# A fused cross-attention, MLA and expert kernel: the queries' RMS factor applied in the softmax's scale, and a new order inside the MLA's head pairs

## The chip, the cores and the metric

The kernel runs on one core of a Trainium2 chip, as one program. The metric is the device time of one execution in microseconds, the median of three runs. The engines are TensorE (PE in the rows, with its weight loads as PEld), VectorE (DVE), ScalarE (ACT), GpSimd (POOL) and SyncE (SP), which issues most transfers. Each runs its own list of instructions in order, and they wait for one another on semaphores.

## The reference

`x` is 256 x 512. Three blocks follow one another, each with a layer norm in front and added to `x`: cross-attention over 4096 rows of context, a multi-head latent attention (MLA) with 16 causal heads, and a mixture of 48 kept experts. The change lies in the MLA, but for one instruction:

```python
q_lat = rms_norm(h @ w_qa.T, q_a_ln_w)              # 384 wide, one factor per row
kv = h @ w_kva.T                                    # 128 latent + 64 rotary
c = rms_norm(kv[..., :128], kv_a_ln_w)              # 128 wide, one factor per row
q = (q_lat @ w_qb.T)                                # per head 128 plain + 64 rotary
k_nope, v = split(c @ w_kvb.T)                      # per head 128 and 128
scores = (q_nope @ k_nope.T + rope(q_pe) @ rope(k_pe).T) * 192 ** -0.5
out = softmax(causal(scores)) @ v                   # then @ w_o.T, all heads
```

The factor of `rms_norm` is `rsqrt(mean(x * x) + eps)` of the row. Queries are rows of the scores, so a factor of a query's latent is a factor of that row of the scores.

## The kernel before

Products in fp32 are made of fp16 halves: an operand is scaled and rounded to a high half (mostly by ScalarE), the remainder is the low half (mostly VectorE, which waits for the high one), and TensorE adds three products, high-high, low-high and high-low.

*Opening.* The first transfers bring key weights `wk32` and context, chunk by chunk. ScalarE rounds chunk c (L471, semaphore `wk_hi`), VectorE makes the low half (`split_wk`), TensorE begins with chunk 0. Somewhat later `transpose_rows` (L1280) turns the normalised `x`, for which it waits for VectorE's L807. Cross-attention follows until 304 us; its exponentials are L531 and L577, whose bias and scale are both columns in SBUF.

*Latents.* The rows are two tiles, t = 0 and 1, of 128 tokens. `latents(t, ...)` writes 384 query and 128 key columns of a tile into one PSUM bank `lat_raw[t]`. ScalarE squares both parts with a sum (L609, L611, `ssq_ready`), VectorE adds epsilon (`add_eps`, L1043), POOL raises both columns to -0.5 (L439), behind the power of the tile's layer norm (L436), and `norm_latents` multiplies the raw latents with factor and weight, the query part in L1047 and the key part in L1049. Between these VectorE rotates the shared rotary keys (`rotate_keys`, L1033 and L1037). TensorE turns latents and keys (`turn_latents` L1512, `turn_keys` L1518), ScalarE and VectorE split the turned latents (L673, L1055). The projections of the first pair, `first_part(t, low, n)`, have n = 0 keys, 1 rotary queries and 2 plain queries; the queries of tile 0 (18 of 66 products) stand ahead of `turn_latents(1)`. Their results are evacuated by L663 (keys), L654 (queries), L1075 and L659 (rotary), with the low halves on VectorE in the order keys L1089, queries L1084, rotary L1080. The scores of pair 0 wait for all of them.

*Pairs.* The 16 heads are 8 pairs; pairs 0 to 6 are `mla_pair`, pair 7 is `mla_last_pair`. TensorE does for pair m: scores into `pO`; projections of pair m + 1 (queries and rotary, keys); six output products of pair m - 1 for tile 0 into `pD` (`out_product(..., 0)`); values of m + 1; six transposes of the probabilities (L1657), which wait for `p_ready`; six output products of pair m - 1 for tile 1 into `pP`; the weighted values, which wait for `pt_ready`. VectorE does: mask (L1103), row maximum (L1107, L1108), its negative times the scale (L1110), low half of the next key weights (L905), in pairs 4 to 6 the low half of an expert unit (L1094), reciprocal (L1116) and product with the probabilities (L1120), rotary product of the next queries (L1075), low halves (L1084, L1089, L1080), low half of the output weights (L1128), low half of the query weights two pairs ahead (L899), low half of the outputs (L1133). ScalarE does: next key weights (L511), four exponentials with row sums (L618), evacuation of the next queries and keys (L654, L663), output weights (L639), rotary high half (L659), evacuation of the turned probabilities (L625), query weights two pairs ahead (L506), outputs (L648) and values (L668), in pairs 3 to 5 also an expert unit's high half for the next pair (L687). In pair 0 alone (`start=True`) the output weights stand behind the turned probabilities. SP loads query weights and output weights of later pairs after `mkv_lo` and `wo_lo`.

Of the kernel before, what the change touches and what calls it, by code (L numbers as in the profile page):

```python
# [12 lines left out]
T, HID = 256, 512  # L13
# [34 lines left out]
def build(nc, a, out):  # L48
# [4 lines left out]
    with ctx:  # L53
# [66 lines left out]
        def take(n, dt=f32):  # L120
# [51 lines left out]
        epsv = take(TT)  # L172
        xsum = take(TT)
# [19 lines left out]
        latc = arena[:, pm_at:pm_at + TT * LAT].rearrange("p (t n) -> p t n", t=TT)  # L193
        kcos, ksin = (arena[:, woh_at + 256 * i:woh_at + 256 * i + 256].rearrange("p (t i d) -> p t i d", t=TT, i=2)
# [59 lines left out]
            wl_hi wl_lo bo_hi bo_ready xsq_ready xl1_ready lat_mm kpe_mm kpn_ready kpe_hi kpe_tr ssq_ready lvar_ready lrstd_ready latn_ready lat_tr lat_hi lat_lo mq_hi mq_lo mkv_hi mkv_lo kpe_ready  # L254
# [130 lines left out]
        def _(pool):  # L385
# [51 lines left out]
            for t in range(TT):  # L437
                pool.wait_ge(s["lvar_ready"], t + 1)
                pool.tensor_tensor(lrs[:, t], ssq[:, t], nhalf[:, :], ALU.pow).then_inc(s["lrstd_ready"], 1)  # L439
# [6 lines left out]
        def _(act):  # L446
# [22 lines left out]
            for c in range(HC):  # L469
                act.wait_ge(first_in[c], 32)  # L470
                act.activation(wk16[:, 0, c], wk32[:, c], ACT.Copy, scale=SW).then_inc(s["wk_hi"], 1)  # L471
# [155 lines left out]
            def mla_pair(m, p, proj=True, ahead=True, start=False):  # L627
# [6 lines left out]
                if start:  # L634
                    rope_hi(m + 1, 1 - p)
                    turned(m)
# [43 lines left out]
            mla_evac_k(0, 0, 1)  # L680
            mla_evac_q(0, 0, 3)
            rope_hi(0, 0)
# [1190 lines left out]
```

## Time and profile before

| | us |
|---|---|
| median of 3 runs (716.0 to 716.07) | 716.04 |
| the profiled execution, its own time | 716.18 |
| its span in the profile | 714.3 |
| TensorE busy | 700.1 (98%) |
| VectorE busy | 610.9 (86%) |
| ScalarE busy | 439.0 (61%) |
| POOL busy | 11.6 (2%) |

The granted clock of TensorE is 1.00 in every stretch shown below. A row of a timeline gives the start and the length in us, the engine, the line, the operation with output and inputs and, in brackets, how long the engine had been idle and who released it. Matmul ends are modelled, so that a matmul row's length holds a tail under which the next may start. A window row gives the stretch, its length, and busy time and instructions of PE, PEld, DVE, ACT and POOL in this order.

### The profile page before, as it was taken

The numbers are of one execution on the slowest core, as the hardware profiler recorded it, in microseconds if no ns is written. First come the engines' busy times: TensorE is split into PE (matmuls) and PEld (weight loads), VectorE is DVE, ScalarE is ACT, GpSimd is POOL, SyncE is SP. The second block draws the span as 40 slices with busy tenths as digits, with TensorE's granted clock in tenths as the row PEclk, the third lists the DMA queues.
The fourth block names the chain that finished last, engine by engine and source line by source line (L and its number), as shares of the span: only waits on it lengthen the run. The fifth ranks groups of instructions, "written<-read, shape, count | busy, mean of one in ns | idle before, by whom it ended". The sixth has DMA issues, their size and how long they took to land.

```text
span 714.3 us, 20505 instructions
## 1 busy us (share of the span) xinstructions
PE 700.1 (98%) x8725; PEld 455.7 (64%) x8725; DVE 610.9 (86%) x950; ACT 439.0 (61%) x610; POOL 11.6 (2%) x36
## 2 busy tenths in 40 slices
PE   8999999999999998998999999999999999999998
PEld 3555555555555554546777767777777777777775
DVE  5679999999999999877889977888888888888885
ACT  4778888787878887735677753444444344444442
POOL 3000000000000000010000000000000000000000
PEclk9999999999999999999999999999999999999999
DMA  8570101010110000032334403678777776777770
GB/s 322 175 276 3 62 3 62 3 61 10 54 25 39 3 3 3 3 128 98 112 121 155 161 1 105 224 215 250 220 246 222 242 239 227 245 225 243 230 238 32
DMA packets 29880, 94.44 MB, mean 132 GB/s; under 512 B 5824, under 2 KB 15088, under 8 KB 28400
## 3 DMA queue, kind: packets, MB, share of 16 engines
q1 hardware_dynamic: 28944, 92.31, 39.2%
q8 instruction: 57, 0.93, 0.6%
q10 hardware_dynamic: 864, 1.07, 0.4%
q14 instruction: 15, 0.12, 0.1%
HBM read 92.76 MB, written 0.57 MB: 131 GB/s over the span
## 4 chain that ended last, share of the span: by engine, by line
PE 91%; ACT 3%; DVE 3%; DMA 1%; issue 1%; POOL 0%; ACTq 0%; DVEq 0%
PE pS L1268 40%; PE pP L1268 30%; PE pO L1268 12%; PE pD L1268 8%; ACT arena L577 2%; DMA arena<-in_ctxT 1%; PE pO L1657 1%; ACT arena L618 0%; DVE xn L1183 0%; DVE xn L807 0%; POOL arena L439 0%; DVE bn L800 0%; DVE arena L1075 0%; DVE arena L790 0%; DVE arena L780 0%
## 5 line engine op out<-in xcount | busy, mean ns | idle before, releaser
L1268 PE MATMUL pS<-arena 128*128 128x256 f16 (+3 forms) x2185 | 253.5, 272 | 1.4 <-ACT arena L708 0.5
L1268 PEld LDWEIGHTS pS<-arena 128*128 128x128 f16 (+1 forms) x2185 | 213.4, 101 | 45.5 <-ACT arena L625 1.9
L1268 PE MATMUL pP<-arena 128*32 128x512 f16 (+1 forms) x2996 | 239.8, 380 | 0.2 <-ACT arena L471 0.2
L1268 PEld LDWEIGHTS pP<-arena 128*32 128x32 f16 (+1 forms) x2996 | 109.0, 97 | 102.0 <-issue 2.2
L531 ACT ACTIVATE arena<-pS,mblk 128x1024 f32<-128x1024 f32 x112 | 128.9, 1206 | 4.9 <-PE pS L1268 4.7
L1094 DVE SCALAR_TENSOR_TENSOR arena<-arena 128x1536 f16<-128x1536 f32 x72 | 126.1, 1752 | 0.8 <-ACT arena L687 0.8
L729 ACT ACTIVATE arena<-pS 128x256 f32<-128x256 f32 x72 | 27.6, 383 | 154.2 <-PE pS L1268 154.2
L1268 PE MATMUL pO<-arena 128*32 128x256 f32 (+6 forms) x1370 | 106.6, 357 | 1.7 <-DVE arena L1080 1.4
L687 ACT ACTIVATE arena<-arena 128x1536 f16<-128x1536 f32 x72 | 106.3, 1477 | 1.0 <-PE pP L1268 1.0
L936 DVE TENSOR_SCALAR arena<-arena 128x1024 f32<-128x1024 f32 x112 | 73.1, 689 | 7.0 <-ACT arena L531 7.0
L1268 PE MATMUL pD<-arena 128*128 128x512 f16 x288 | 77.8, 379 | 0.0
L1268 PEld LDWEIGHTS pO<-arena 128*32 128x32 f32 (+3 forms) x1370 | 47.4, 106 | 39.0 <-issue 15.5
L1229 DVE TENSOR_TENSOR arena<-pS,arena 128x256 f32<-128x256 f32 x72 | 30.6, 425 | 36.4 <-ACT arena L729 36.4
L1268 PE MATMUL pS<-work,arena 32*128 32x256 f16 x1536 | 53.4, 269 | 3.5 <-ACT arena L577 3.1
L1268 PEld LDWEIGHTS pS<-work,arena 32*128 32x128 f16 x1536 | 33.8, 93 | 32.8 <-issue 26.2
L1268 PEld LDWEIGHTS pD<-arena 128*128 128x128 f16 x288 | 28.2, 98 | 17.1 <-DVE arena L1242 0.2
L1238 DVE TENSOR_TENSOR arena<-arena 128x256 f32<-128x256 f32 x68 | 29.0, 426 | 7.1
L460 ACT ACTIVATE arena<-pP,xb 128x512 f16<-128x512 f32 x29 | 19.9, 687 | 24.3 <-PE pP L1268 24.3
L945 DVE TENSOR_TENSOR x_sb<-x_sb,arena 128x1024 f32<-128x1024 f32 x26 | 31.8, 1223 | 1.7 <-DVE x_sb L945 0.5
L945 DVE TENSOR_TENSOR arena<-arena 128x1024 f32<-128x1024 f32 x26 | 31.8, 1223 | 1.4
L945 DVE TENSOR_TENSOR xT<-xT,arena 128x1024 f32<-128x1024 f32 x26 | 31.8, 1222 | 1.4
L945 DVE TENSOR_TENSOR xn<-xn,arena 128x1024 f32<-128x1024 f32 x26 | 31.8, 1222 | 1.4
(260 smaller groups left out, 527.9 us busy)
## 6 DMA issues: line engine op xcount, KB each, us to landing
arena<-in_units SPq DMA_DIRECT2D x72, 768.0 KB, 5.0
arena<-w_scratch SPq DMA_DIRECT2D x136, 64.0 KB, 2.7
arena<-in_ctxT SPq DMA_DIRECT2D x7, 1024.0 KB, 5.3
mw_in<-in_mla_in SPq DMA_DIRECT2D x8, 832.0 KB, 6.8
mw_out<-in_mla_out SPq DMA_DIRECT2D x8, 512.0 KB, 3.8
wlatT<-in_wlatT SPq DMA_DIRECT2D x1, 1280.0 KB, 10.7
arena<-in_wkT SPq DMA_DIRECT2D x4, 256.0 KB, 5.4
arena<-in_ctxT ACTq DMA_DIRECT2D x4, 256.0 KB, 6.4
```

What stands on the lines that cost most here:

```text
L460: act.activation(kh[:, p, n], bank, ACT.Identity, bias=xb[:, 1, n:n + 1], scale=1.0 / SW)
L531: act.activation(probs[:, tile], step_scores(st), ACT.Exp, bias=mblk[:, p, 1, tile:tile + 1], scale=mblk[:, p, 0, tile:tile + 1])\
L577: act.activation(probs[:, tile], step_scores(st), ACT.Exp, bias=mblk[:, p, 1, tile:tile + 1], scale=mblk[:, p, 0, tile:tile + 1])\
L687: act.activation(uwh[:, slot], uw32[:, slot], ACT.Copy, scale=SW).then_inc(s["unit_hi"], 1)
L729: act.activation(sg[:, buf], pS[:, bank, 0:T], ACT.Silu, scale=1.0 / (SA * SW)).then_inc(s["silu_ready"], 1)
L936: dve.tensor_scalar(probs[:, t], probs[:, t], LO, HI, ALU.max, ALU.min).then_inc(s["clip_done"], 1)
L945: dve.tensor_tensor(acc, acc, probs[:, t], ALU.add).then_inc(s["sum_done"], 1)
L1094: dve.scalar_tensor_tensor(uwl[:, slot], uw32[:, slot], SW, uwh[:, slot], ALU.mult, ALU.subtract).then_inc(s["unit_lo"], 1)
L1229: dve.tensor_tensor(m1[:, buf], pS[:, bank, T:2 * T], sg[:, slot], ALU.mult).then_inc(s["m1_ready"], 1)
L1238: dve.tensor_tensor(m2[:, buf], m1[:, buf], wb[:, slot], ALU.mult).then_inc(s["m2_ready"], 1)
L1268: return pe.matmul(o, lhsT, rhs, start=start, stop=stop, **kw)
L1657: last = pe.transpose(pO[:, j, 128 * i:128 * i + 128], pm[:, j, 128 * i:128 * i + 128], ident[:, :])
```

## The change

1. The first chunk of the key weights is rounded in two halves, and TensorE waits for the second ahead of its third product only.
2. The query latents are no longer multiplied with their RMS factor. The key part's sum, factor and product stand alone (`kv_squares`, `kv_latents`, one column on POOL); the query part is multiplied with the norm's weight only (`q_latents`). The query sum of tile 1 is taken after the latents are turned. One POOL power for both tiles gives the factors, and `q_scales` makes two columns of them per tile, with the softmax's scale and with its negative. The exponentials take the first as their scale, and the negative maximum is the maximum times the second.
3. Both tiles of latents are turned ahead of all first-part products. Their order is then: all high products of tile 0, its low ones; in tile 1 rotary, keys, queries. Evacuations and low halves follow this order.
4. In every pair ScalarE splits the output weights behind the turned probabilities, as pair 0 did.
5. In pairs 1 to 6 the first of the six output products for tile 1 stands in front of the wait for the probabilities and of the transposes.

Not shown: the new tiles and semaphore names, the thresholds of `wk_hi` raised by one, and the same replacements in the last pair.

```diff
-                pool.tensor_tensor(lrs[:, t], ssq[:, t], nhalf[:, :], ALU.pow).then_inc(s["lrstd_ready"], 1)
+                pool.tensor_tensor(lrs[:, t, 1:2], ssq[:, t, 1:2], nhalf[:, 0:1], ALU.pow).then_inc(s["lrstd_ready"], 1)
+            pool.wait_ge(s["qvar_ready"], 1)
+            pool.tensor_tensor(lrs[:, :, 0], ssq[:, :, 0], nhalf[:, :], ALU.pow).then_inc(s["qrs_ready"], 1)
...
-                act.activation(wk16[:, 0, c], wk32[:, c], ACT.Copy, scale=SW).then_inc(s["wk_hi"], 1)
+                if c == 0:
+                    act.activation(wk16[:, 0, 0, 0:256], wk32[:, 0, 0:256], ACT.Copy, scale=SW).then_inc(s["wk_hi"], 1)
+                    act.activation(wk16[:, 0, 0, 256:512], wk32[:, 0, 256:512], ACT.Copy, scale=SW).then_inc(s["wk_hi"], 1)
+                else:
+                    act.activation(wk16[:, 0, c], wk32[:, c], ACT.Copy, scale=SW).then_inc(s["wk_hi"], 1)
...
-            for t in range(TT):
+            def kv_squares(t):
                 act.wait_ge(s["lat_mm"], t + 1)
-                act.activation(latc[:, t, 0:QLR], lat_raw[t][:, 0:QLR], ACT.Square, scale=float(QLR) ** -0.5 / (SX * SW),
-                               accum_out=ssq[:, t, 0:1])
-                act.activation(latc[:, t, QLR:LAT], lat_raw[t][:, QLR:LAT], ACT.Square, scale=float(KVLR) ** -0.5 / (SX * SW),
-                               accum_out=ssq[:, t, 1:2]).then_inc(s["ssq_ready"], 1)
+                act.activation(lat_sq[:, t, QLR:LAT], lat_raw[t][:, QLR:LAT], ACT.Square, scale=float(KVLR) ** -0.5 / (SX * SW),
+                               accum_out=ssq[:, t, 1:2]).then_inc(s["kvsq_ready"], 1)
+
+            def q_squares(t):
+                act.activation(lat_sq[:, t, 0:QLR], lat_raw[t][:, 0:QLR], ACT.Square, scale=float(QLR) ** -0.5 / (SX * SW),
+                               accum_out=ssq[:, t, 0:1]).then_inc(s["qsq_ready"], 1)
+
+            kv_squares(0)
+            q_squares(0)
+            kv_squares(1)
...
-                                              scale=S_SCALE, accum_out=sm[:, t, j:j + 1])
+                                              scale=qsc[:, t, 0:1], accum_out=sm[:, t, j:j + 1])
...
-            def mla_pair(m, p, proj=True, ahead=True, start=False):
+            def mla_pair(m, p, proj=True, ahead=True):
                 if proj:
                     split_kv(m + 1, 1 - p)
                 mla_exps(m)
                 if proj:
                     mla_evac_q(m + 1, 1 - p)
                     mla_evac_k(m + 1, 1 - p)
-                if start:
                     rope_hi(m + 1, 1 - p)
-                    turned(m)
+                turned(m)

                 act.wait_ge(mout_in[p], 16 * (m // 2 + 1) if isinstance(m, int) else 8 * (m - p) + 16)
                 act.activation(woh[:, p], mw_out[:, p], ACT.Copy, scale=SW).then_inc(s["wo_hi"], 1)
-                if not start:
-                    if proj:
-                        rope_hi(m + 1, 1 - p)
-                    turned(m)
                 if ahead:
                     split_q(m + 2, p)
...
-            mla_evac_k(0, 0, 1)
+            act.wait_ge(s["latn_ready"], 3)
+            q_squares(1)
+            mla_evac_k(0, 0, 2)
+            rope_hi(0, 0)
             mla_evac_q(0, 0, 3)
-            rope_hi(0, 0)
             split_q(1, 1)
             mla_evac_v(0, 0)
...
-            mla_pair(0, 0, start=True)
-            mla_pair(1, 1)
-            with act.Fori(2, PAIRS - 5, 2) as m:
+            with act.Fori(0, PAIRS - 5, 2) as m:
                 mla_pair(m, 0)
                 mla_pair(m + 1, 1)
...
-                dve.wait_ge(s["ssq_ready"], t + 1)
-                dve.tensor_scalar(ssq[:, t], ssq[:, t], epsv[:, t:t + 1], None, ALU.add).then_inc(s["lvar_ready"], 1)
-
-            def norm_latents(t):
+                dve.wait_ge(s["kvsq_ready"], t + 1)
+                dve.tensor_scalar(ssq[:, t, 1:2], ssq[:, t, 1:2], epsv[:, t:t + 1], None, ALU.add).then_inc(s["lvar_ready"], 1)
+
+            def q_latents(t):
+
+                dve.wait_ge(s["qsq_ready" if t == 0 else "kvsq_ready"], t + 1)
+                dve.tensor_tensor(latc[:, t, 0:QLR], lat_raw[t][:, 0:QLR], lnw_b[:, 0:QLR], ALU.mult)                   .then_inc(s["latn_ready"], 1)
+
+            def kv_latents(t):
                 dve.wait_ge(s["lrstd_ready"], t + 1)
-                dve.scalar_tensor_tensor(latc[:, t, 0:QLR], lat_raw[t][:, 0:QLR], lrs[:, t, 0:1], lnw_b[:, 0:QLR],
-                                         ALU.mult, ALU.mult).then_inc(s["latn_ready"], 1)
                 dve.scalar_tensor_tensor(latc[:, t, QLR:LAT], lat_raw[t][:, QLR:LAT], lrs[:, t, 1:2], lnw_b[:, QLR:LAT],
                                          ALU.mult, ALU.mult).then_inc(s["latn_ready"], 1)
+
+            def q_scales():
+
+                dve.wait_ge(s["qrs_ready"], 1)
+                for o, f in ((qsc, S_SCALE), (nqsc, -S_SCALE)):
+                    last = dve.tensor_scalar(o, lrs[:, :, 0:1].broadcast_to([128, TT, 2]), f, None, ALU.mult)
+                link(last)
...
-            norm_latents(0)
+            q_latents(0)
+            kv_latents(0)
             rotate_keys(1)
             add_eps(1)
+            q_latents(1)
+            kv_latents(1)
             lo_latents(0)
-            norm_latents(1)
             dve.wait_ge(s["kpe_hi"], 1)
             dve.scalar_tensor_tensor(kpel, kpeT, SH / (SX * SW), kpeh, ALU.mult, ALU.subtract).then_inc(s["kpe_ready"], 1)
             lo_latents(1)
+            dve.wait_ge(s["qsq_ready"], TT)
+            dve.tensor_tensor(ssq[:, :, 0], ssq[:, :, 0], epsv[:, :], ALU.add).then_inc(s["qvar_ready"], 1)
...
-                dve.tensor_scalar(nm, mx, -S_SCALE, None, ALU.mult).then_inc(s["negmax"], 1)
+                dve.tensor_tensor(nm, mx, nqsc, ALU.mult).then_inc(s["negmax"], 1)
...
-            rope_mul(0, 0, 2)
+            rope_mul(0, 0, 1)
             lo_k(0, 0, 1)
+            rope_lo(0, 0)
             lo_q(0, 0, 2)
-            rope_lo(0, 0)
+            q_scales()
             split_q(1, 1)
...
                     for n in range(HC):
+                        if c == 0 and k == 0 and n == 2:
+                            pe.wait_ge(s["wk_hi"], 2)
...
+                for i in products:
+                    j, (x, w) = i // 3, ((ah, woh), (ah, wol), (al, woh))[i % 3]
+                    done = mm((pD, pP)[t][:, :], x[:, j, 128 * t:128 * t + 128], w[:, p, HID * j:HID * j + HID],
+                              False, False, skip_group_check=True)
                 return done
...
+                if before:
+                    out_product(m - 1, 1 - p, 1, products=range(1))
                 pe.wait_ge(s["p_ready"], m + 1)
                 for j in range(2):
                     for i in range(3):
                         last = pe.transpose(pO[:, j, 128 * i:128 * i + 128], pm[:, j, 128 * i:128 * i + 128], ident[:, :])
                 last.then_inc(s["pt_done"], 1)
                 if before:
-                    out_product(m - 1, 1 - p, 1)
+                    out_product(m - 1, 1 - p, 1, products=range(1, 6))
                 else:
                     residual(1)
...
-            first_part(0, False, 2)
-            first_part(0, True, 2)
             turn_latents(1)
-            for n in (1, 0):
+            for low in (False, True):
+                for n in (1, 0, 2):
+                    first_part(0, low, n)
+            for n in (1, 0, 2):
                 for low in (False, True):
-                    first_part(0, low, n)
-            for low in (False, True):
-                for n in (0, 1, 2):
                     first_part(1, low, n)
```

## Rows read from the trace of the kernel before

**Rows 1.** The page, part 1: busy us (share of the span) xinstructions.
```profile
PE 700.1 (98%) x8725; PEld 455.7 (64%) x8725; DVE 610.9 (86%) x950; ACT 439.0 (61%) x610; POOL 11.6 (2%) x36
```

**Rows 2.** Busy time by stretch: us long, then per engine; granted clock; DMA share, GB/s.
```profile
312.00:331.58 19.58, 17.15 (x146) 10.92 (x145) 13.94 (x39) 9.19 (x24) 3.33 (x6) 1.00 0.52 205
331.58:342.43 10.85, 10.41 (x98) 8.28 (x99) 7.92 (x17) 6.71 (x16) 0.00 (x0) 1.00 0.01 2
353.49:364.49 11.00, 11.00 (x103) 8.65 (x101) 9.22 (x20) 7.61 (x17) 0.00 (x0) 1.00 0.38 125
375.49:386.74 11.25, 11.25 (x104) 8.53 (x102) 10.58 (x19) 8.99 (x18) 0.00 (x0) 1.00 0.34 123
409.21:422.93 13.72, 11.91 (x88) 6.79 (x86) 11.01 (x33) 6.97 (x16) 1.11 (x2) 1.00 0.01 1
```

**Rows 3.** Timeline of the opening: start, us, engine, line, operation, [idle before <-releaser].
```profile
16.15 1.07 PE L1280 MATMUL pS<-ident,xn 128*128 128x128 f32 x8 [0.83 <-DVE xn L807]
```

**Rows 4.** Timeline, the latents' norms.
```profile
320.93 0.22 DVE L1043 TENSOR_SCALAR arena<-arena 128x2 f32<-128x2 f32 x1
321.09 0.55 POOL L436 TENSOR_TENSOR rstd<-var,nhalf 128x1 f32<-128x1 f32 x1 [2.19 <-DVE var L1025]
322.34 0.62 DVE L1047 SCALAR_TENSOR_TENSOR arena<-pO,arena 128x384 f32<-128x384 f32 x1 [1.19 <-POOL arena L439]
322.88 0.34 DVE L1049 SCALAR_TENSOR_TENSOR arena<-pO,arena 128x128 f32<-128x128 f32 x1
324.31 0.44 PE L1518 MATMUL pO<-ident,arena 128*128 128x128 f32 x2 [0.43 <-DVE arena L1037]
```

**Rows 5.** Timeline, from the first projections to the scores of pair 0.
```profile
326.37 2.87 PE L1268 MATMUL pS<-arena 128*128 128x128 f16 x48
328.94 0.69 DVE L1075 SCALAR_TENSOR_TENSOR arena<-pS,arena 128x512 f32<-128x512 f32 x1 [1.05 <-PE pS L1268]
329.28 0.60 ACT L654 ACTIVATE arena<-pS 128x512 f16<-128x512 f32 x1
330.75 0.68 DVE L1080 TENSOR_TENSOR arena<-arena 128x512 f16<-128x512 f32 x1
331.58 2.35 PE L1268 MATMUL pO<-arena 128*128 128x128 f16 x36 [1.42 <-DVE arena L1080]
```

**Rows 6.** Timeline of pair 0, up to the mask of pair 1.
```profile
338.91 0.68 DVE L1075 SCALAR_TENSOR_TENSOR arena<-pS,arena 128x512 f32<-128x512 f32 x1
340.17 0.79 ACT L625 ACTIVATE arena<-pO 128x768 f32<-128x768 f32 x1
341.01 1.57 PE L1268 MATMUL pS<-arena 128*128 128x256 f32 x8 [0.23 <-ACT arena L625]
341.94 1.23 DVE L1128 SCALAR_TENSOR_TENSOR arena<-mw_out,arena 128x1024 f16<-128x1024 f32 x1 [0.55 <-ACT arena L639]
344.95 0.76 DVE L1103 TENSOR_TENSOR pO<-pO,cmask 128x256 f32<-128x256 f32 x2
```

**Rows 7.** Timeline of pair 2.
```profile
359.69 0.18 DVE L1116 RECIPROCAL arena<-arena 128x4 f32<-128x4 f32 x1 [1.16 <-ACT arena L618]
361.23 0.82 PE L1657 MATMUL pO<-ident,arena 128*128 128x128 f32 x6
362.09 0.81 ACT L625 ACTIVATE arena<-pO 128x768 f32<-128x768 f32 x1
```

**Rows 8.** Timeline of pair 4, with an expert unit's split.
```profile
380.42 1.75 DVE L1094 SCALAR_TENSOR_TENSOR arena<-arena 128x1536 f16<-128x1536 f32 x1
383.36 0.64 PEld L1657 LDWEIGHTS pO<-ident,arena 128*128 128x128 f32 x6 [0.24 <-DVE arena L1120]
```

**Rows 9.** Single lines of ScalarE: ns min/median/max of one, starts, forms.
```profile
L466 ACT ACTIVATE arena<-pP x29: 597/597/643, 30.1 to 279.0; 128x512 f32<-128x512 f32 x29
L460 ACT ACTIVATE arena<-pP,xb x29: 684/687/688, 20.3 to 261.5; 128x512 f16<-128x512 f32 x29
L531 ACT ACTIVATE arena<-pS,mblk x112: 1192/1207/1230, 35.1 to 276.5; 128x1024 f32<-128x1024 f32 x112
```

More of the change, by code:

```diff
@@ L172, in build @@
         epsv = take(TT)
+        qsc, nqsc = (take(2 * TT).rearrange("p (t j) -> p t j", t=TT) for _ in range(2))
         xsum = take(TT)
@@ L193, in build @@
         latc = arena[:, pm_at:pm_at + TT * LAT].rearrange("p (t n) -> p t n", t=TT)
+        lat_sq = arena[:, pm_at + TT * LAT:pm_at + 2 * TT * LAT].rearrange("p (t n) -> p t n", t=TT)
         kcos, ksin = (arena[:, woh_at + 256 * i:woh_at + 256 * i + 256].rearrange("p (t i d) -> p t i d", t=TT, i=2)
@@ L253, in build @@
             last_pv den_read inverted rows_done dsq_ready wo_sums wo_ready bo_ready0 ctx_mul ctxn_ready delta_done
-            wl_hi wl_lo bo_hi bo_ready xsq_ready xl1_ready lat_mm kpe_mm kpn_ready kpe_hi kpe_tr ssq_ready lvar_ready lrstd_ready latn_ready lat_tr lat_hi lat_lo mq_hi mq_lo mkv_hi mkv_lo kpe_ready
+            wl_hi wl_lo bo_hi bo_ready xsq_ready xl1_ready lat_mm kpe_mm kpn_ready kpe_hi kpe_tr kvsq_ready qsq_ready lvar_ready lrstd_ready qvar_ready qrs_ready latn_ready lat_tr lat_hi lat_lo mq_hi mq_lo mkv_hi mkv_lo kpe_ready
             mproj_done qkv_ready qk_lo rope_mul rope_hi rope_ready s_done masked maxed negmax exps_done rec_ready p_ready
@@ L702, in mla_last_pair @@
                         last = act.activation(pm[:, j, lo:hi], tail_s[t][:, j, :], ACT.Exp, bias=nm[:, t, j:j + 1],
-                                              scale=S_SCALE, accum_out=sm[:, t, j:j + 1])
+                                              scale=qsc[:, t, 0:1], accum_out=sm[:, t, j:j + 1])
                     last.then_inc(s["exps_done"], 1)
@@ L788, in split_wk @@
             def split_wk(n):
-                dve.wait_ge(s["wk_hi"], n + 1)
+                dve.wait_ge(s["wk_hi"], n + 2)
                 dve.scalar_tensor_tensor(wk16[:, 1, n], wk32[:, n], SW, wk16[:, 0, n], ALU.mult, ALU.subtract)\
@@ L823, in _ @@
             for c in range(HC):
-                dve.wait_ge(s["wk_hi"], HC + c + 1)
+                dve.wait_ge(s["wk_hi"], HC + c + 2)
                 dve.scalar_tensor_tensor(wv16[:, 1, c], wv32[:, c], SW, wv16[:, 0, c], ALU.mult, ALU.subtract)\
@@ L1152, in mla_last_pair @@
                     dve.wait_ge(s["maxed"], m + 1 + t)
-                    dve.tensor_scalar(nm[:, t], mx[:, t], -S_SCALE, None, ALU.mult).then_inc(s["negmax"], 1)
+                    dve.tensor_tensor(nm[:, t], mx[:, t], nqsc[:, t], ALU.mult).then_inc(s["negmax"], 1)
                 for t, (lo, hi) in enumerate(((0, 128), (128, 384))):
@@ L1328, in _ @@
                     if k == 0:
-                        pe.wait_ge(s["wk_hi"], c + 1)
+                        pe.wait_ge(s["wk_hi"], c + 2 if c else 1)
                         pe.wait_ge(s["ctx_hi"], c + 1)
@@ L1590, in proj_v, with out_product @@
                 last.then_inc(s["mproj_done"], 1)
-            def out_product(m, p, t, last=False):
+            def out_product(m, p, t, last=False, products=range(6)):
                 if t == 0:
@@ L1597, in out_product @@
                     pe.wait_ge(s["a_lo"], m + 1 + (t if last else 0))
-                for j in range(2):
-                    for k, (x, w) in enumerate(((ah, woh), (ah, wol), (al, woh))):
-                        done = mm((pD, pP)[t][:, :], x[:, j, 128 * t:128 * t + 128], w[:, p, HID * j:HID * j + HID],
-                                  False, False, skip_group_check=True)
+                for i in products:
+                    j, (x, w) = i // 3, ((ah, woh), (ah, wol), (al, woh))[i % 3]
+                    done = mm((pD, pP)[t][:, :], x[:, j, 128 * t:128 * t + 128], w[:, p, HID * j:HID * j + HID],
+                              False, False, skip_group_check=True)
                 return done
```

## The prediction

> **What bounds the kernel now.** I read the page first: TensorE is busy for 98% of the span [rows 1], so only its stalls, or work taken from it, can move the time. The change takes no product away. I therefore cut the stretch that the diff touches at the starts of the score products, 331.58, 342.43, 353.49, 364.49, 375.49, 386.74, 397.97 and 409.21 us, and looked at each part in the busy time by stretch [rows 2]: 19.58 us of preparation, of which TensorE works 17.15; pair 0 takes 10.85; pair 1 takes 11.06 (342.43 to 353.49); pairs 2 and 3 take 11.00 with TensorE full; pairs 4 to 6, in which ScalarE and VectorE split an expert unit besides, take 11.25, 11.23 and 11.24. Seven pairs: 77.63 us. Then I read the timeline of each part for who is late. All sums are for the profiled execution, 716.18 us (a span of 714.3 and 1.88 outside it), which is 0.14 above the median of 716.04.
>
> **The opening** (first weight split in two halves). TensorE starts 0.25 earlier at best, but at 16.15 us it has been idle for 0.83 us, waiting for the normalised x [rows 3], and that comes from VectorE, which hangs on x's transfer and statistics, not on this split. 0.83 covers 0.25 either way, a delay of the low half by the second ScalarE instruction (0.1) too. Zero; without the cover it would be plus or minus 0.25.
>
> **Latents to first scores.** Before, the factors of both RMS norms go through POOL together. VectorE's instruction for rows 0 waits for POOL's two powers that begin at 321.09, and runs at 322.34; its key part follows at 322.88 and the rotation of the keys behind that, so the keys' transposes come at 324.31, with TensorE idle for 0.43 [rows 4]. After: the query part needs no factor and fits behind the sums of 320.93, in the time in which POOL works. POOL's power on one column is 0.55 [rows 4], so both powers end at 321.09 + 0.55 + 0.55 = 322.19. Key part then instead of at 322.88: 0.69 earlier, and so the rotation and, at 323.62, the key transposes. Then rows 1, by the same durations: sum 323.49, query part 323.56 to 324.18, POOL 323.69 to 324.24, key part 324.27 to 324.61, last transpose 324.66. TensorE now has all 66 first-part products behind it, from 324.77. Before, the last 48 of them take 2.87 from 326.37 with the tail of the last one, 2.71 or 0.0565 each without it, and ScalarE takes the query block at 329.28, 0.20 after that [rows 5]. After: 324.77 + 66 x 0.0565 = 328.50, query block at 328.70. The high and low halves of the latents (ScalarE 324.99 to 325.59, VectorE 325.72 to 326.41) are ready before rows 1 want them at 326.63. ScalarE's postponed query squares (0.37 and a read) fit at 325.48 to 326.05, ahead of the first block at 327.68.
>
> The order of the blocks also counts. Before, rotary, keys and queries came within 0.4 us, and VectorE's four instructions (rotary at 328.94, the last at 330.75 for 0.68) kept the scores waiting for 1.42 us, to 331.58 [rows 5]. After: 33 + 9 products give the rotary block at 324.77 + 2.37 + 0.20 = 327.34, keys 327.68, queries 328.70. VectorE: rotary 327.34 to 328.03, low keys 328.32, low rotary 328.92, low queries 329.52 to 330.20; scores 0.15 behind, 330.35. That is **1.23 us earlier**. The two new scale columns (two instructions like the 0.22 of the sums) come behind the last of these and ahead of a weights' split that waits for ScalarE's half anyway: zero. If one of these hand-overs is late, TensorE's line is the floor for the loss: the gain would be between 0 and 1.4.
>
> **The exponentials' scale becomes a column.** No row has this instruction. Near ones [rows 9]: a copy of 128x512 out of PSUM takes 0.597 us, with a bias column 0.687, so a column costs 0.09. The cross-attention's exponential has a bias and a scale column and takes 1.207 on 1024 columns; copies grow from 0.597 (512) to 0.792 (768) [rows 6], so 1024 would be about 0.99 to 1.02, and two columns cost 0.19 to 0.22. I take 0.10 for each exponential, **0.40 for a pair's four**. Bounds: 0 (the second column read beside the first) and 0.20. The Trainium skill, page "ScalarE: Activation LUTs", section "What ACT_TABLE_LOAD costs", says that every [128,1] pointer operand adds about 93 ns. By that rule, an estimate, a pair's four cost 0.37 rather than 0.40, and the 28 of pairs 0 to 6 would cost 2.6 us if nothing hid them; the 1.207 agrees with its 186 + 0.833 x 1024 + 2 x 93 = 1225 ns.
>
> Nothing hides them in the light pairs: VectorE's reciprocal at 359.69 has waited 1.16 us for the exponentials [rows 7]. The chain from there is visible in pair 0 [rows 6]: rotary product on VectorE at 338.91 (7.33 after the scores' start), evacuation of the turned probabilities at 340.17 (+1.26, behind the rotary high half), weighted values at 341.01 (+0.84), next scores at 342.43 (+1.42). Pair 0 gets 0.40 longer: **11.25**.
>
> **Weights' split behind the turned probabilities.** Pair 0 already has this order, so its rows price it. From the evacuation at 340.17: high weights behind it, low weights on VectorE at 341.94, for which VectorE had idled 0.55; behind these the next query weights' low half and the low outputs; and only at 344.95, 4.78 after the evacuation and 2.52 after the scores' start, the mask of pair 1 [rows 6]. In the other pairs ScalarE does the weights while it waits for VectorE, and VectorE is idle when the scores end, so the mask comes 0.04 behind their 2.35 [rows 5], 2.39 after their start. The moved instruction thus fills the turn of VectorE, and its queue behind it (query weights, low outputs, mask, maximum, reciprocal) waits. Pairs 1 to 6 after the change: mask 2.52, 0.13 late; rotary product 7.33 + 0.13 + 0.40 = 7.86; evacuation 9.12; weighted values 9.96; next scores **11.38**; and the next mask again 9.12 + 4.78 - 11.38 = 2.52, so that it repeats. In pairs 4 to 6 the reciprocal follows the unit's split (380.42, which holds VectorE 1.67: 6.60 after the scores; +0.13 = 6.73 [rows 8]); the exponentials come 359.69 - 353.49 + 0.13 + 0.40 = 6.73: the same, so 11.38 too. The transfers of later weights, which SP issues behind this low half, are issued a little later and are due most of a pair later, zero; so are their uses on ScalarE, which move with them. The maximum's product with a column for one with a constant is 4 elements wide: zero, 0.05 a pair at most.
>
> **One output product ahead of the transposes.** TensorE waited here for the normalised probabilities in the unit pairs (its weight load idled 0.24 [rows 8]), 0.13 over its own pace, which is that of pair 2: 361.23 - 353.49 = 7.74 [rows 7]. One of six products of 0.22 fills that. But the weighted values then wait for the evacuation, which hangs on the rotary chain above, not on the transposes: with 7.74, the product's 0.22 and 0.07 for the key weights' low half behind the late mask they start at 8.03, and 0.86 later (362.09 after 361.23) the evacuation could run, at 8.89; it runs at 9.12. Zero where 9.12 holds; without the chain it would give 0.13 in three pairs, and cost about 0.07 in the others, where five products no longer cover the evacuation.
>
> **Sum.** Preparation -1.23. Pairs: 11.25 + 6 x 11.38 = 79.53 against 77.63, +1.90. In the last pair, only the second group's two exponentials are on the path (0.20, half of it under products): +0.10. Together +0.77: 716.95 in the profile's terms, **716.8** against the median.
>
> **The rivals.** *The column is free.* Then pairs 1 to 3 are set by TensorE with small waits (11.13, 11.14, 11.14) and pairs 4 to 6 by the late mask (11.37): 78.37, +0.74, and the whole -0.49: 715.5. For it: an engine could read both columns at once. Against: 1.207. *Slower: the latents' wait takes the place of the projections.* Both rows' latents are now turned before any first-part product, where 18 products used to cover POOL's second power. If the factors of rows 1 come 1.2 us later than my 324.66, the whole preparation gain is gone and only the pairs' +2.0 stays: 718.0. It decides the sign from 0.65 late on. An exponential of 0.20 more instead (pairs at 11.78) would even give 719.8. *Faster: the pairs run at TensorE's own pace.* If VectorE does not get late, 10.85 + 6 x 11.00 = 76.85, -0.78, and with the preparation -2.0: 714.0. For it: pairs 2 and 3 have slack, and pairs 4 to 6 lose 0.25 each that the product ahead aims at. Against: 344.95, where the very order shows a late mask.
>
> **How the numbers follow.** A measurement of this kernel can tell 0.2%, 1.43 us, from no change. The forecast (716.8, own range 715.8 to 717.7) gets 0.60, the free column 0.12, the slower ones 0.17, the faster one 0.11. The forecast's upper edge passes 717.5 with about 0.04. So faster 0.12, same 0.67, slower 0.21. The range for 8 in 10 leaves out the faster case and the far end of the slower: 715.0 to 718.2.
>
> **What will show it.** First scores at 330.35 rather than 331.58; key transposes at 323.6. Pairs all near 11.38, also 1 to 3. Exponentials of 0.46 to 0.56 and 0.37 to 0.47. The mask 2.52 after the scores, with VectorE idle ahead of the low output weights, not of the mask. If pairs 1 to 3 stay at 11.0 to 11.1, the column price or the rotary chain is wrong; if the first scores come after 331, the preparation is.

## The result, and the profile after

The changed kernel takes **717.63 us** (median of 14 runs, 717.5 to 717.93), the kernel before 716.06 (14 runs, 715.85 to 716.53): a ratio of 1.0022, with a 95% interval of 1.0014 to 1.0029. That is +1.57 us where +0.77 was forecast, inside the stated range (715.0 to 718.2), at the upper edge of the forecast's own (715.8 to 717.7), and just beyond the 1.43 us from which I called a difference measurable. The profiled execution after took 717.5 with a span of 715.7 (before: 716.18 and 714.3).

The page of the kernel after, part 1 (busy us, share, instructions), to be read against [rows 1]:

```profile
PE 701.7 (98%) x8725; PEld 455.0 (64%) x8725; DVE 610.8 (85%) x953; ACT 441.3 (62%) x611; POOL 12.0 (2%) x37
```

ScalarE does 2.3 us more work, and the product count is the same. The same stretches as in [rows 2], cut at the starts of the scores, in the kernel after:

```profile
311.61:330.21 18.60, 17.03 (x145) 10.94 (x144) 13.89 (x42) 9.18 (x24) 3.74 (x7) 1.00 0.56 216
330.21:341.42 11.21, 10.41 (x98) 8.27 (x99) 8.00 (x17) 6.97 (x16) 0.00 (x0) 1.00 0.00 0
352.75:364.08 11.33, 11.33 (x103) 8.52 (x101) 9.16 (x19) 7.87 (x18) 0.00 (x0) 1.00 0.35 123
375.42:386.78 11.36, 11.35 (x103) 8.47 (x101) 10.71 (x20) 9.24 (x19) 0.00 (x0) 1.00 0.33 122
409.50:423.37 13.87, 12.06 (x88) 6.80 (x85) 11.63 (x33) 7.23 (x16) 1.09 (x2) 1.00 0.00 1
```

Preparation is 0.98 shorter (18.60 for 19.58), pair 0 takes 11.21 for 10.85, pair 2 takes 11.33 for 11.00, pair 4 takes 11.36 for 11.25, the last pair 0.15 more. The scores start at 330.21, 341.42, 352.75, 364.08, 375.42, 386.78, 398.14 and 409.50: 79.29 us for seven pairs, +1.66.

**The opening** came out 0.39 earlier. Timeline of the kernel after, against [rows 3]:

```profile
9.10 0.63 ACT L479 ACTIVATE arena<-arena 128x512 f16<-128x512 f32 x1 [1.63 <-DMA arena<-in_ctxT]
...
14.22 1.39 DVE L816 TENSOR_SCALAR xn<-x_sb,mv,rstd 128x512 f32<-128x512 f32 x2
...
15.76 1.07 PE L1304 MATMUL pS<-ident,xn 128*128 128x128 f32 x8 [0.38 <-DVE xn L816]
```

A chunk of context landed 0.39 earlier (ScalarE takes it at 9.10; the kernel before at 9.49), and the normalised x with it. Numbers 1, 2 and 7 below, whose openings hold the same instructions as this kernel's, take it at 8.99, 9.56 and 8.93. Numbers 3 and 4, which run the programs of before and after unchanged, take it 0.23 and 0.28 later than those did (9.72 and 9.38). So the runs don't show it to be an effect of the split in halves.

**Latents**, timeline of the kernel after, against [rows 4, 5]:

```profile
321.21 0.55 POOL L441 TENSOR_TENSOR arena<-arena,nhalf 128x1 f32<-128x1 f32 x1
...
321.80 0.35 DVE L1061 SCALAR_TENSOR_TENSOR arena<-pO,arena 128x128 f32<-128x128 f32 x1 [0.59 <-POOL arena L441]
...
323.25 0.44 PE L1544 MATMUL pO<-ident,arena 128*128 128x128 f32 x2 [0.16 <-DVE arena L1046]
...
323.93 0.79 PE L1538 MATMUL pO<-ident,arena 128*128 128x128 f32 x4 [0.24 <-DVE arena L1057]
...
324.55 3.85 PE L1292 MATMUL pS<-arena 128*128 128x128 f16 x66
...
328.45 0.59 ACT L663 ACTIVATE arena<-pS 128x512 f16<-128x512 f32 x1
...
329.27 0.68 DVE L1107 SCALAR_TENSOR_TENSOR arena<-pS,arena 128x512 f16<-128x512 f32 x1
...
330.21 1.04 PE L1292 MATMUL pO<-arena 128*128 128x128 f16 x20 [0.90 <-DVE arena L1107]
```

With 0.39 added, to have the clock of the kernel before, the key transposes start at 323.64 (forecast 323.62), the 66 products at 324.94 (324.77), the query block at 328.84 (328.70), the low queries at 329.66 (329.52), the scores at 330.60 (330.35). From POOL's power for rows 0 to the first scores, numbers 4, 9 and 12, which have all of this preparation, gain 0.97 or 0.98 too.

**Pairs**, timeline of the kernel after from the end of pair 0 into pair 1 (what [rows 6, 7] show of before):

```profile
340.93 1.23 DVE L1151 SCALAR_TENSOR_TENSOR arena<-mw_out,arena 128x1024 f16<-128x1024 f32 x1 [0.55 <-ACT arena L652]
...
341.42 2.36 PE L1292 MATMUL pO<-arena 128*128 128x128 f16 x36
...
343.94 0.75 DVE L1126 TENSOR_TENSOR pO<-pO,cmask 128x256 f32<-128x256 f32 x2
...
345.99 0.46 ACT L632 ACTIVATE arena<-pO,arena 128x128 f32<-128x128 f32 x1 [2.55 <-DVE arena L1133]
...
346.43 0.56 ACT L632 ACTIVATE arena<-pO,arena 128x256 f32<-128x256 f32 x1
...
348.10 0.18 DVE L1139 RECIPROCAL arena<-arena 128x4 f32<-128x4 f32 x1 [1.55 <-ACT arena L632]
...
349.24 0.69 DVE L1098 SCALAR_TENSOR_TENSOR arena<-pS,arena 128x512 f32<-128x512 f32 x1
...
350.49 0.79 ACT L639 ACTIVATE arena<-pO 128x768 f32<-128x768 f32 x1
...
351.34 1.57 PE L1292 MATMUL pS<-arena 128*128 128x256 f32 x8
...
352.75 2.36 PE L1292 MATMUL pO<-arena 128*128 128x128 f16 x36
```

The mask starts 2.52 after the scores, VectorE has idled 0.55 ahead of the low output weights and not ahead of the mask, the reciprocal waits 1.55 for the exponentials (1.16 before), and from the rotary product the chain runs as forecast: evacuation 1.25 later, weighted values 0.85 after that, next scores 1.41 after those.

**The end.** From the last pair on the kernel after is 0.44 late, constantly: -0.39 - 0.98 + 1.66 + 0.15. Its last store is issued at 712.21, before at 711.77. Yet the span grew by 1.36. SyncE's waits from 700 us on (us in total, times, longest) and the issues there (count, KB, us from issue to landing), first the waits and the transfers of the kernel before, then the waits and the transfers (queue packets, MB and share included) of the kernel after:

```profile
SPq L53 <- DMA out<-work: 1.8, 1, 1.8
```

```profile
out<-work SPq DMA_DIRECT2D x2, 256.0 KB, 2.1
```

```profile
SPq L53 <- DMA out<-work: 2.7, 1, 2.7
```

```profile
q14 instruction: 1, 0.01, 0.1%
...
out<-work SPq DMA_DIRECT2D x2, 256.0 KB, 2.8
```

So 0.9 us is lost after the last instruction of every engine, in the final store. The records of single packets show the same 288 packets of the store spread over 2.30 instead of 1.51 us, and one packet of 8 KB of queue q14, which the page names an instruction queue, 1.01 us after the store's first packet; in the kernel before it comes 4.06 us after it, when the store has landed. No step of the prediction looked there.

### The profile page after: what moved, and what is told of

Its sections match the earlier page's. It is cut to its first block, busy times and chain, and to the rows that moved or that the text cites. A ratio compares the mean times of both kernels' runs of the same rounds, so it can differ in the third digit from the quotient of the medians.

```text
span 715.7 us, 20535 instructions
## 1 busy us (share of the span) xinstructions
PE 701.7 (98%) x8725; PEld 455.0 (64%) x8725; DVE 610.8 (85%) x953; ACT 441.3 (62%) x611; POOL 12.0 (2%) x37
## 4 chain that ended last, share of the span: by engine, by line
PE 91%; ACT 4%; DVE 3%; DMA 1%; issue 1%; POOL 0%; ACTq 0%; DVEq 0%
PE pS L1292 40%; PE pP L1292 29%; PE pO L1292 12%; PE pD L1292 8%; ACT arena L585 2%; DMA arena<-in_ctxT 1%; PE pO L1685 1%; ACT arena L632 0%; DVE xn L1207 0%; DVE xn L816 0%; DVE bn L809 0%; DVE arena L799 0%; DVE arena L1042 0%; DVE arena L789 0%; ACT arena L711 0%
```

## The experiments

Each is measured beside runs of the kernel before on the same chip, whose median is given with it. Intervals are those of the ratio. The pairs' sum is from the first scores to those of pair 7.

**1. The constant scale again.** The order and everything else stay. The kernel leaves the queries' factor out of the exponentials, so it doesn't compute the reference; its instructions are the same in number. The last pair's exponentials are changed in the same way.

```diff
-                                              scale=qsc[:, t, 0:1], accum_out=sm[:, t, j:j + 1])
+                                              scale=S_SCALE, accum_out=sm[:, t, j:j + 1])
```

> The kernel after, but the exponentials take the softmax's scale as a constant again (the queries' RMS factor is left out of them; the maximum is still multiplied with its column). If the column's 0.10 us for each exponential stands on the chain of a pair, as forecast, the scores of pairs 0 to 7 start 0.4 us closer together in pair 0 (10.8 instead of 11.21 us), pairs 1 to 3 come to 11.1 and pairs 4 to 6 stay near 11.35, since VectorE's unit split sets their chain: together 0.9 to 1.0 us less, about 716.7. If only the place of the output weights' split made the pairs longer, nothing changes: 717.6.

716.66 us against 716.12 (1.0009, 1.0 to 1.0018), 0.97 less than the changed kernel. Timeline of this build in pair 1:

```profile
345.53 0.37 ACT L632 ACTIVATE arena<-pO,arena 128x128 f32<-128x128 f32 x1 [2.54 <-DVE arena L1133]
...
345.89 0.46 ACT L632 ACTIVATE arena<-pO,arena 128x256 f32<-128x256 f32 x1
...
347.28 0.18 DVE L1139 RECIPROCAL arena<-arena 128x4 f32<-128x4 f32 x1 [1.18 <-ACT arena L632]
...
351.63 1.22 DVE L1151 SCALAR_TENSOR_TENSOR arena<-mw_out,arena 128x1024 f16<-128x1024 f32 x1 [0.73 <-ACT arena L652]
...
354.64 0.75 DVE L1126 TENSOR_TENSOR pO<-pO,cmask 128x256 f32<-128x256 f32 x2
```

Exponentials of 0.37 and 0.46 for 0.46 and 0.56, and the wait is back at 1.18. The column costs 0.09 to 0.10 for each. Pairs 0 to 3 take 10.85, 11.15, 11.18 and 11.15, so the path pays all four columns in pair 0 (0.36) and about half of them (0.15 to 0.18) in pairs 1 to 3. Pairs 4 to 6 stay at 11.36 to 11.37. The sum is 78.42, 0.87 less than 79.29. The last pair, too, is back at its length before, 0.15 less. The free-column rival had forecast pairs within 0.04 of these (11.13, 11.14, 11.37), so its arithmetic holds and only its premise fell. The Trainium skill, page "ScalarE: Activation LUTs", section "What ACT_TABLE_LOAD costs", gives about 93 ns for each [128,1] pointer operand; the rows agree.

**2. The output weights ahead again.** In all pairs ScalarE splits them before the rotary high half and the evacuation, pair 0 too.

```diff
+                act.activation(woh[:, p], mw_out[:, p], ACT.Copy, scale=SW).then_inc(s["wo_hi"], 1)
                 if proj:
                     rope_hi(m + 1, 1 - p)
                 turned(m)
-                act.activation(woh[:, p], mw_out[:, p], ACT.Copy, scale=SW).then_inc(s["wo_hi"], 1)
```

> The kernel after, but ScalarE splits the output weights ahead of the rotary high half and of the turned probabilities, in every pair. If the late mask (2.52 us after the scores' start instead of 2.39) lengthens every pair by its delay, pairs 1 to 6 come to 11.24 instead of 11.33 to 11.36 and the mask to 2.39: 0.6 us less, 717.0. If the order costs nothing because the columns alone set the chain, nothing changes: 717.6. If the order was the main cost, the pairs fall to 11.0: 2 us less, 715.6.

717.02 against 716.12 (1.0013, 1.0004 to 1.0023). The sum of the pairs is 78.56, 0.73 less than 79.29, with pairs of 11.20 to 11.25. The timed difference to the changed kernel is 0.61, less than that by 0.12; with scatters of 0.2 to 0.3 in the opening the runs can't say why.

**3 and 4. Empty instructions that are not in the program.** Both were meant to shift VectorE's list of instructions and with it the instruction packet, by instructions that do nothing.

```diff
+            for _ in range(4):   # 60 in the other
+                dve.nop()
             dve.wait_ge(first_in[0], 32)
```

> The kernel before with four empty VectorE instructions at its start, where VectorE waits for the first transfer anyway. In the profile after, one packet of 8 KB of the second instruction queue falls between the packets of the last store and the store's last packets on one DMA engine come about 0.9 us late; before, such a packet came after the store. If VectorE's instruction list, four longer after the change, is what moves it, this kernel gets 0.9 to 1.1 us slower than before with all engines' work unmoved: 717.1. If it is another engine's list, nothing changes: 716.1.

> The kernel after with 60 empty VectorE instructions at its start, to move the place in the list at which code is fetched away from the end. If VectorE's list moves the packet that falls into the last store, it goes, and the kernel is 0.9 to 1.1 us faster than after: 716.6. If not, 717.6, or slower by what the 60 instructions delay the first use of VectorE.

716.09 (1.0002, 0.9993 to 1.0011) and 717.63 (1.0021, 1.0012 to 1.003), against 716.12. The programs that ran hold none of these instructions, so the lists were those of the kernels before and after, and the packet lies 4.05 and 1.02 us behind the store's first, as there. The two are no test, only a repetition, and they repeat both times. Their profiles show how far two executions of one program differ: the first scores come at 331.80 (before: 331.58) and 330.51 (after: 330.21).

**5 and 6. Instructions that stay.** With an increment of a semaphore that nobody reads they stay in the program. In 5 they stand in ScalarE's list, in 6 in VectorE's, both in the changed kernel.

```diff
+            for _ in range(40):
+                act.nop().then_inc(s["pad_a"], 1)
```
```diff
+            for _ in range(60):
+                dve.nop().then_inc(s["pad_d"], 1)
```

> The kernel after with 40 instructions more at the start of ScalarE's list, each of which only raises an unused semaphore, in the time in which ScalarE waits for the first transfers. (In the two runs before, the empty VectorE instructions were dropped when the program was built, so their lists were those of the kernels before and after; they tell the scatter and nothing of the packet.) ScalarE's list got 5 shorter in the change. If its length puts the 8 KB packet of the second instruction queue into the last store, the packet moves, the store's packets span 1.5 us instead of 2.3 and the kernel takes 0.8 to 1.1 us less, 716.7. If another engine's list does it, 717.6.

> The same with 60 instructions more at the start of VectorE's list, and none on ScalarE. If VectorE's list, 4 longer after the change, places the packet: 716.7 and a store of 1.5 us. If ScalarE's does: 717.6 and a store of 2.3 us.

Number 5: 719.89 (five runs) against 715.91 (1.0055, 1.0042 to 1.0069). The packet stays 1.01 us behind the store's first and the store takes 2.30, so it is not ScalarE's. What made it slower is another thing: ScalarE loads its table behind the added instructions. Timeline of this build:

```profile
5.62 1.28 ACT L478 ACT_TABLE_LOAD   x1 [5.62 <-issue]
...
7.38 0.39 PE L1294 MATMUL pP<-arena 128*128 128x512 f16 x1 [1.58 <-ACT arena L478]
```

The table load is at 5.62 instead of 2.90, the first product at 7.38 instead of 5.64, and the first scores come 1.25 later (331.46). That is all of the 1.2 by which this span is longer. The profiled execution was the fastest (718.76); the others went up to 720.36, and why is open.

Number 6: 716.88 against 715.91 (1.0021, 1.0012 to 1.003). The packet moves to 35.6 us ahead of the store, and the store takes 1.50. So the packet carries VectorE's instructions and the store gets its 0.8 back. The time itself came in two groups, six of 11 runs at 716.73 to 716.88 and five at 718.24 to 718.75; the profile is from the second (first scores at 332.34; VectorE's first split starts at 6.41 instead of 5.07), and the runs don't say what makes the groups. The median 716.88 is the upper end of the first group and says little by itself. A smaller number of added instructions was wanted.

**7. No product ahead of the transposes.**

```diff
-                    out_product(m - 1, 1 - p, 1, products=range(1))
...
-                    out_product(m - 1, 1 - p, 1, products=range(1, 6))
+                    out_product(m - 1, 1 - p, 1)
```

> The kernel after with all six output products of tile 1 behind the transposes, as before. If the weighted values wait for the rotary chain through ScalarE, as forecast, the product ahead buys nothing: pairs 11.33 to 11.36 as in the kernel after, 717.6. If it fills the wait for the probabilities and that wait counts, the pairs get up to 0.13 longer each: up to 718.4.

717.5 against 715.91 (1.0022, 1.0013 to 1.0031); the pairs sum to 79.26, against 79.29, and keep 11.33 and 11.36. The product ahead is worth nothing while the rotary chain sets the evacuation, as the prediction had it.

**8. The kernel before with the order of the blocks alone.** Projections of tile 1, evacuations and low halves in the order rotary, keys, queries.

```diff
-                for n in (0, 1, 2):
-                    first_part(1, low, n)
+                for n in (1, 0):
+                    first_part(1, low, n)
+            for low in (False, True):
+                first_part(1, low, 2)
...
-            mla_evac_k(0, 0, 1)
-            mla_evac_q(0, 0, 3)
-            rope_hi(0, 0)
+            mla_evac_k(0, 0, 2)
+            rope_hi(0, 0)
+            mla_evac_q(0, 0, 3)
...
-            rope_mul(0, 0, 2)
+            rope_mul(0, 0, 1)
             lo_k(0, 0, 1)
-            lo_q(0, 0, 2)
             rope_lo(0, 0)
+            lo_q(0, 0, 2)
```

> The kernel before with one thing of the change: in tile 1 rotary and keys are projected ahead of the queries, and evacuated and split in that order. The RMS factors, the scale of the exponentials and the pairs stay as before. From the rows of before, the last low half ends near 331.0 instead of 331.43: the first scores 0.4 to 0.5 us earlier, pairs unchanged at 77.6, and the packet behind the store: 715.6. If the later low halves of the latents stall the products instead, 716.1.

715.62 against 715.91 (0.9996, 0.9987 to 1.0005): by the intervals no difference. In the profile the scores come at 330.90 for 331.58, of which 0.37 was gained in the stretches before the latents; 0.31 is the blocks' order. TensorE's wait ahead of the scores is 0.94 for 1.42 [rows 5]. The expectation was 0.4 to 0.5; the scores start 0.26 behind the end of the low queries (329.96 + 0.68 to 330.90), where they had started 0.15 behind that of the low rotary half. So of the 0.98 that the latents gained, about a third is this order. By difference, two thirds are left for the factor that is no longer waited for and the latents turned together; these two were not tried apart.

**9 and 10. A few VectorE instructions more.** 24 in the changed kernel, to bring the packet away from the store; 4 in the kernel before, to bring it into the store. (The diff is that of number 6, with 24 and 4.)

> The kernel after with 24 instructions more at the start of VectorE's list, few enough to end before VectorE's first transfer lands at 5.1 us. If the place of the 8 KB packet is all that the last store pays, the packet moves ahead of the store, the opening stays, and the kernel takes 0.8 to 1.0 us less than after: 716.7. If the 60 of before gained in another way, 717.6.

> The kernel before with four instructions more at the start of VectorE's list, the number that the change adds. If that number brings the packet into the last store, it lies 1.0 us behind the store's first packet here too, the store's packets span 2.3 us instead of 1.5, and this kernel takes 0.8 to 1.0 us more than before with no other work changed: 716.9. If the change's packet comes from something else in its list, 716.0.

Number 9: 716.73 against 715.89 (1.0011, 1.0002 to 1.0021), which is 0.90 less than the changed kernel (0.73 less, when each is taken against the kernel before on its chips). Number 10: 716.40 against 715.89 (1.0007, 0.9998 to 1.0017), +0.51 where +0.9 was expected. The stores, by the single packets (us):

```
                 span     store: first to last packet   q14's last packet, from the store's first
before          714.331   1.51                          +4.06
before + 4      714.790   2.30                          +1.02
after           715.686   2.30                          +1.01
after + 24      715.229   1.51                          -13.47
after + 60      716.899   1.50                          -35.59
```

Waits of the build "before + 4" and then of "after + 24", from 700 us on:

```profile
SPq L53 <- DMA out<-work: 2.7, 1, 2.7
```

```profile
SPq L53 <- DMA out<-work: 1.8, 1, 1.8
```

Four instructions that compute nothing put the 0.9 us into the kernel before, and 24 take it out of the changed one. All fourteen profiles agree: from the first normalisation behind the last pair (422.07 before, 422.51 after) to the end of the span it is 293.17 or 293.18 us in the seven whose packet falls into the store (the changed kernel, numbers 1, 2, 4, 5, 7 and 10), and 292.26 to 292.30 in the seven others. That number 10 lost only 0.5 in all is in its profile too: its first scores are at 331.15, 0.43 ahead of before, gained not in the opening (x's transposes at 16.12, [rows 3]: 16.15) but in two steps of about 0.2 near 220 and 247 us, in the cross-attention, where both kernels have the same instructions. What gives and takes such steps stays open; they are as large as the differences below 0.5 us in these comparisons.

**11 and 12. The parts put together.** 11 has the constant scale, the weights ahead and 24 instructions more, and again leaves out the queries' factor; 12 is the same with the column, and so computes all of the reference.

> The kernel after with the exponentials' scale as a constant (the queries' factor is left out of them), the output weights' split ahead again, and the 24 instructions. If column, order and packet are all that the change costs, the pairs come to 77.6 to 77.7 us as before and only the preparation's gain of 1.0 stays: 715.0 to 715.1. If more is hidden, over 715.5.

> The kernel after with the output weights' split ahead again and the 24 instructions, nothing left out. The pairs at 78.56 as in the run with the weights first, the store at 1.5 us: 717.0 - 0.9 = 716.1, the same as before.

Number 11: **714.92** against 715.89 (0.9988, 0.9978 to 0.9997): with column, order and packet gone, -0.97 is left. Its first scores start at 329.98, and its pairs take 10.87, 11.09, 11.09, 11.10, 11.23, 11.24 and 11.24, together 77.86. So the forecast of 77.6 to 77.7 for the pairs was missed by 0.2: the preparation's gain of 0.98, less 0.23 in the pairs, gives -0.75, and the other 0.2 of the measured time is no larger than the differences in stretches that both kernels share. Number 12: **715.88** against 715.89 (0.9999, 0.999 to 1.0009), 1.75 less than the changed kernel and the same as before. Its mask, in the timeline:

```profile
351.49 1.22 DVE L1154 SCALAR_TENSOR_TENSOR arena<-mw_out,arena 128x1024 f16<-128x1024 f32 x1
...
352.61 2.36 PE L1295 MATMUL pO<-arena 128*128 128x128 f16 x36
...
355.00 0.76 DVE L1129 TENSOR_TENSOR pO<-pO,cmask 128x256 f32<-128x256 f32 x2 [0.42 <-PE pO L1295]
```

Low output weights without a wait of VectorE ahead of them, and the mask 2.39 after the scores, with VectorE idle: on time. From the first scores to the first normalisation behind the last pair this build takes 91.54 (330.20 to 421.74), the kernel before 90.49, number 11 90.72 and the changed kernel 92.30. So from number 11 to 12 the column adds 0.82 (0.96 by the medians), from 12 to the changed kernel the place of the weights' split adds 0.76, and 0.23 is left that is neither: 0.02 to 0.03 in pairs 0 and 1, 0.09 in each of pairs 2 and 3.

## Why the prediction was right, and where it was short

| step | forecast | after, by the profile |
|---|---|---|
| opening | 0 | -0.39 |
| latents to first scores | -1.23 | -0.98 |
| seven pairs | +1.90 | +1.66 |
| last pair | +0.10 | +0.15 |
| last store | no step | +0.9 |
| sum | +0.77 | +1.36 in the span |

**The latents.** Right in mechanism: key transposes where forecast, the wait of TensorE in front of them 0.16 for 0.43, rotary, keys and queries in order. A quarter of a microsecond was lost in three hand-overs. POOL's power for rows 1 began 0.10 late; behind the key part the last transpose and the projections took 0.07 longer; and the scores begin 0.26 after the low queries' end, where I had taken the 0.15 that lies behind the low rotary half in [rows 5]. Number 8, which also ends with the low queries, has the same 0.26.

**The pairs.** The chain of pair 0, read from [rows 6] and put into all pairs, was right: 2.52 for the mask as forecast, pairs of 11.33 to 11.36 for 11.38, 11.21 for 11.25 in pair 0. Of the 0.24 by which the sum was too high, 0.16 fits the price of the column: 0.36 and not 0.40 a pair, 0.04 in each of pairs 0 to 3. The column can't explain the 0.02 in each of pairs 4 to 6, which keep their length without it. That nothing hides the columns in the light pairs was too strong: in pairs 1 to 3 their absence gives back 0.15 to 0.18 of the 0.36, and only pair 0 gives back all. Numbers 1 and 2 take out one cost at a time, 0.87 for the column and 0.73 for the order. The two overlap and can't be added: number 11, without either, has pairs of 77.86, so together they cost 1.43 of the 1.66, and the other 0.23 is neither. That pairs 4 to 6 keep their length without the column was not in the forecast's words, but in its rival's (11.37): there the column is hidden behind the unit's split and the late mask decides.

**The product ahead.** Forecast zero where the rotary chain sets the evacuation: shown by number 7. Forecast +0.07 in the pairs without that chain: number 11 has 11.09 and 11.10 in pairs 2 and 3 against 11.00, and 11.23 and 11.24 in pairs 4 to 6 where 0.13 of gain was priced but did not come. Of the 0.23, 0.18 lie in pairs 2 and 3. That it is the product which costs the 0.09 was not tried apart.

**The opening.** The prediction said zero, by the 0.83 of cover. It came out 0.39 earlier by a transfer's landing, which varies by 0.2 to 0.3 between two executions of the same program; whether the change has a part in it can't be said. In the median it is worth less than in this profile: without it the terms give -0.98 + 1.66 + 0.15 + 0.9 = 1.73, with it 1.34, and 1.57 was measured.

**What failed** is the claim, made by leaving it out, that behind the last pair nothing changes. The sum went by the work and the waits of the kernel; the 0.9 us came from where the instructions lie. Without it the result would have been near the forecast of 716.8: number 9, which is the changed kernel without it, took 716.73. That this comes so close is in part luck, since two misses cancel: the preparation gained 0.25 less than forecast and the pairs lost 0.24 less. And the result lies inside the stated range only because the range was wide enough for a cost that no sentence of the prediction names. The slower rival (the latents' wait in the place of the projections, 718.0) came near in time and was wrong: the projections start within 0.2 of the forecast.

## What to carry to other kernels

A factor moved into another instruction's operand isn't free if that instruction is on the path: here 0.09 us an exponential took back 0.8 to 1.0 us (numbers 12 against 11, and the changed kernel against 1), and at most some 0.7 us had been gained where the factor stood. Before an order is used everywhere, read its price where it already stands: pair 0's mask, 2.52 after the scores, told together with the column's price the length of all pairs to within 0.05 us. And when a time differs by less than 1 us, compare the stretch behind the last computation too, and repeat the build with a few instructions more, before the difference is put down to the change.

## What the runs showed of the hardware

**An instruction packet in the last store costs 0.9 us.** The packet is 8 KB, on the instruction queue q14, and comes where VectorE's list puts it: 4 more instructions bring it 3.0 us earlier, 24 more 14.5, 60 more 36.6, while 40 more of ScalarE's leave it in its place. Within the store it stretches 1.51 us to 2.30. The Trainium skill, page "Runtime: NRT & Kernel Launch", section "Instruction fetch mechanics", says that a sequencer fetches its instructions by a DMA queue of its own and that the cost of crossing a block is mostly hidden. Of the first, the rows show that packets follow an engine's own list, but not that the queue is its own: number 5 moves another packet of q14 from 515.7 to 481.9 us, so ScalarE's instructions come on it too. The second doesn't hold for the one packet that falls into the kernel's last transfer; what the others cost no run here tells. How the packet holds the store up by more than its own 0.31 us was not resolved. In the changed kernel the next slow packets of the store take 0.13, 0.27 and 0.22 us, where the others around them take 0.08, and from 1.9 us after the first the last ones come singly, 0.08 apart.

**Equal instructions don't run equally to 0.4 us.** A context chunk was taken up between 8.93 and 9.56 us in kernels with the same opening, and 0.23 and 0.28 apart in two executions of one and the same program (numbers 3 and 4). Number 10 gained 0.4 in a stretch that it shares with the kernel before.
